# Graph attention on one core: softmax batches of 26 steps, a longer ring of values, and keys and values added in two operations

## The reference, cut to what matters

```python
e = (edge_attr @ We).reshape(-1, H, C)
kj = k[src] + e
vj = v[src] + e
logits = jnp.einsum('ehc,ehc->eh', q[dst], kj) / np.sqrt(C)
m = jax.lax.stop_gradient(jax.ops.segment_max(logits, dst, num_segments=n))
ex = jnp.exp(logits - m[dst])
denom = jax.ops.segment_sum(ex, dst, num_segments=n)
a = ex / (denom[dst] + 1e-16)
agg = jax.ops.segment_sum(vj * a[:, :, None], dst, num_segments=n)
return agg.reshape(n, H * C) + x @ Ws + bs
```

## Time and profile before

| | |
|---|---|
| runs | median 5180.2 us of 3 (5168.29 to 5180.98) |
| the profiled execution's own time | 5169.64 us |
| its span in the profile | 5167.9 us |
| busy share of PE, DVE, ACT, POOL over the span | 85%, 81%, 57%, 60% |
| mean busy share of the DMA engines in e2's steady part | 70% |
| steps of e1 (first to last L1268) | 1365.5 to 3077.4 us |
| steps of e2 (first to last L1268) | 3307.2 to 4972.1 us |

### The profile page before, as it was taken

One profiled execution on the slowest core, in us unless ns is written; L12 is line 12 of the kernel. 1 busy time (PEld: TensorE's weight loads), 2 busy tenths in 40 slices (PEclk: granted clock), 3 DMA queues, 4 the chain that ended last, 5 costly groups with the idle time before them and its releaser, 6 DMA issues. The chain is left out here.

```text
span 5167.9 us, 109620 instructions
## 1 busy us (share of the span) xinstructions
PE 4373.5 (85%) x18094; PEld 3309.7 (64%) x18094; DVE 4191.4 (81%) x21620; ACT 2963.0 (57%) x10810; POOL 3098.8 (60%) x2997
## 2 busy tenths in 40 slices
PE   2666666679899999999999988899999999999978
PEld 1444444445577777777777764577777777777755
DVE  5555555568799999999999986799999999999966
ACT  0000000013188888888888883088888888888881
POOL 5777777710466666666666640476666666666620
PEclk9888787789999999999999997999999999999979
DMA  2444444435677776777776753676677667666734
GB/s 70 120 118 117 118 118 118 118 101 169 191 213 209 206 210 204 211 207 214 208 206 205 206 159 121 198 213 208 206 204 207 204 203 207 205 207 206 207 92 149
DMA packets 573602, 911.16 MB, mean 176 GB/s; under 512 B 93619, under 2 KB 400442, under 8 KB 572935
## 3 DMA queue, kind: packets, MB, share of 16 engines
q0 software_dynamic: 171408, 540.40, 36.2%
q1 hardware_dynamic: 401528, 363.76, 23.2%
HBM read 838.88 MB, written 64.92 MB: 175 GB/s over the span
## 5 line engine op out<-in xcount | busy, mean ns | idle before, releaser
L1162 POOL DMA_INDIRECT e_kv<-kv,src x1664 | 1619.5, 973 | 693.6 <-DVE e_kvj L1268 322.9
L1409 ACT ACTIVATE e_vals<-e_kvj,e_ex 128x65 f32<-128x65 f32 x6656 | 1750.3, 334 | 0.0
L1223 PE MATMUL e_sum<-e_vals,e_mask 128*128 128x260 f32 x3328 | 1077.2, 406 | 217.9 <-ACT e_vals L1409 217.6
L1268 DVE TENSOR_TENSOR e_kvj<-e_kv,e_e 128x512 f32<-128x512 f32 x1664 | 1126.5, 677 | 69.3 <-DMA e_kv<-kv,src 30.3
L1278 DVE CUSTOM_DVE_ANT_0 e_kvj<-e_kvj,e_q 128x64 f32<-128x64 f32 x6656 | 1076.7, 218 | 63.3 <-PE e_q L1184 5.7
L1174 PE MATMUL e_e<-e_we,e_ea 112*128 112x256 f32 x3328 | 1007.9, 384 | 31.4 <-DMA e_ea<-attr_tiles 15.5
L1184 PE MATMUL e_q<-q,e_pick 128*128 x3328 | 999.9, 381 | 26.1 <-POOL e_pick L1152 25.9
L1175 PE MATMUL e_e<-e_we,e_ea 112*128 112x256 f32 x3328 | 990.9, 379 | 0.0
L488 PE MATMUL e_sum<-e_x,e_mask 128*128 x1664 | 583.3, 498 | 403.4 <-DMA e_x<-x_rows,e_src 280.9
L466 POOL DMA_INDIRECT e_x<-x_rows,e_src x783 | 741.5, 947 | 262.4 <-issue 178.8
L1152 POOL TENSOR_SCALAR e_pick<-e_spots,own 128x512 f32<-128x512 bf16 x416 | 657.5, 1581 | 399.1 <-DMA e_spots<-locals 391.2
(11 more groups left out here) (213 smaller groups left out, 3209.4 us busy)
## 6 DMA issues: line engine op xcount, KB each, us to landing
e_ea<-attr_tiles SPq DMA_DIRECT2D x1664, 112.0 KB
e_spots<-locals SPq DMA_DIRECT2D x208, 256.0 KB
e_kv<-kv,src POOLq DMA_INDIRECT x1664
kv<-n_proj_rows SPq DMA_DIRECT2D x98, 256.0 KB
n_x<-x_rows SPq DMA_DIRECT2D x98, 128.0 KB
e_x<-x_rows,e_src POOLq DMA_INDIRECT x783
e_pen<-pens SPq DMA_DIRECT2D x416, 8.1 KB
e_block_cols<-x_cols SPq DMA_DIRECT2D x49, 128.0 KB
```

Of the source, the lines that this page charges most:

```text
L1162: e.indirect_dma_start(out=kv[:, u, :], out_offset=None, **rows_of(kv_rows, k["src"][:, i:i + 1])).then_inc(kv_got[u], 16)
L1223: e.matmul(sums[n % 2][:, 0:VALS], mask[:, n % R, :], vals[:, n % R, :], start=True, stop=True).then_inc(summed, 1)
L1268: e.tensor_tensor(kvj[:, ka:va + 1:va - ka, :, 0:C], kv[:, i % NG, :].rearrange("p (t d) -> p t d", t=2).rearrange(by_head_kv, h=H), pe_e[ ...
L1409: by_weight = e.activation(vals[:, n % R, h * HV:(h + 1) * HV], kvj[:, 2 + n % NV, h, :], ACT.Copy, scale=ex[:, b % 2, h, r:r + 1])
```

## The change

In the attention passes it does the following. A softmax batch has 26 steps instead of 16. LAG follows, from 32 to 42. The ring of values has LAG + 2 buffers instead of LAG + 4, so 44 instead of 36. Keys and values are added by two operations of 256 columns each, with semaphores of their own (`kj_done`, `vj_done`); the dot products wait for the first, the gather and the next product for the second. The destinations are loaded in chunks of 4 steps instead of 8, two chunks ahead. `apart` has one buffer instead of two. Outside the passes, the edge weights (needed in setup and e0 only) lie in the space of the queries.

```diff
-BATCH = 16
+BATCH = 26
...
-    weight = sb("weight", [P, S])
...
-    sb("q", [P, B * D])
+    q = sb("q", [P, B * D])
+    weight = k["weight"] = q[:, 0:S]
...
-    CH, QUAD = 8, 4
+    QUAD = 4
     PACE = 2
     LAG = BATCH + 8 * PACE
-    NV, NG, NE, R = LAG + 4, 6, 6, 4
+    NV, NG, NE, R = LAG + 2, 6, 6, 4
...
-        apart = ph.sb("apart", [P, 2, P])
-        spots = ph.sb("spots", [P, 2, CH * P], BF16)
+        apart = ph.sb("apart", [P, P])
+        spots = ph.sb("spots", [P, 2, QUAD * P], BF16)
...
                 def load_spots(c):
                     if c >= 2:
-                        e.wait_ge(picked, (c - 1) * CH // QUAD)
-                    e.dma_start(spots[:, c % 2, :], locals16[c * CH:(c + 1) * CH, :].rearrange("s c -> (s c)").unsqueeze(0)
-                                .to_broadcast([P, CH * P])).then_inc(spots_got[c % 2], 16)
+                        e.wait_ge(picked, c - 1)
+                    e.dma_start(spots[:, c % 2, :], locals16[c * QUAD:(c + 1) * QUAD, :].rearrange("s c -> (s c)").unsqueeze(0)
+                                .to_broadcast([P, QUAD * P])).then_inc(spots_got[c % 2], 16)
...
-                    if i % CH == 4 and i // CH >= 1 and i // CH + 1 < T // CH:
-                        load_spots(i // CH + 1)
+                    if i % QUAD == 0 and i // QUAD + 2 < T // QUAD:
+                        load_spots(i // QUAD + 2)
...
                     if i >= NG:
-                        e.wait_ge(kvj_done, i - NG + 1)
+                        e.wait_ge(vj_done, i - NG + 1)
...
                     if i >= 2:
-                        e.wait_ge(kvj_done, i - 1)
+                        e.wait_ge(vj_done, i - 1)
...
+                    edge = pe_e[i % 2][:, 0:D].rearrange("p (h c) -> p h c", h=H)
+                    e.tensor_tensor(kvj[:, i % 2, :, 0:C], kv[:, i % NG, 0:D].rearrange("p (h c) -> p h c", h=H), edge,
+                                    ALU.add).then_inc(kj_done, 1)
                     if i >= NV:
                         e.wait_ge(weighed, i - NV + 1)
-                    ka, va = i % 2, 2 + i % NV
-                    by_head_kv = "p t (h c) -> p t h c"
-                    e.tensor_tensor(kvj[:, ka:va + 1:va - ka, :, 0:C],
-                                    kv[:, i % NG, :].rearrange("p (t d) -> p t d", t=2).rearrange(by_head_kv, h=H),
-                                    pe_e[i % 2][:, 0:D].unsqueeze(1).to_broadcast([P, 2, D]).rearrange(by_head_kv, h=H),
-                                    ALU.add).then_inc(kvj_done, 1)
-                    e.wait_ge(kvj_done, i + 1)
+                    e.tensor_tensor(kvj[:, 2 + i % NV, :, 0:C], kv[:, i % NG, D:].rearrange("p (h c) -> p h c", h=H), edge,
+                                    ALU.add).then_inc(vj_done, 1)
+                    e.wait_ge(kj_done, i + 1)
...
-                        if n >= 2:
-                            e.wait_ge(masked, n - 1)
-                        e.activation(apart[:, n % 2, :], k["iota"][:], ACT.Square, bias=k["local"][:, n:n + 1],
+                        if n:
+                            e.wait_ge(masked, n)
+                        e.activation(apart[:], k["iota"][:], ACT.Square, bias=k["local"][:, n:n + 1],
```

More of the change, by code:

```diff
@@ L1066, in edge_pass_attention @@
         w_got, cleared, ones_set = ph.sem("w_got"), ph.sem("cleared"), ph.sem("ones_set")
-        e_done, q_done, kvj_done, dots_done, picked, apart_done = (
-            ph.sem(n) for n in ("e_done", "q_done", "kvj_done", "dots_done", "picked", "apart_done"))
+        e_done, q_done, kj_done, vj_done, dots_done, picked, apart_done = (
+            ph.sem(n) for n in ("e_done", "q_done", "kj_done", "vj_done", "dots_done", "picked", "apart_done"))
         flat_done, lr_done, fw_done, mx_inner = (ph.sem(n) for n in ("flat_done", "lr_done", "fw_done", "mx_inner"))
@@ L1147, in pick_rows @@
                 def pick_rows(c):
-                    e.wait_ge(spots_got[c // 2 % 2], 16 * (c // 4 + 1))
+                    e.wait_ge(spots_got[c % 2], 16 * (c // 2 + 1))
                     if c >= 2:
                         e.wait_ge(q_done, (c - 1) * QUAD)
-                    e.tensor_scalar(pick[:, c % 2, :], spots[:, c // 2 % 2, c % 2 * QUAD * P:(c % 2 + 1) * QUAD * P],
-                                    k["own"][:, 0:1], None, ALU.is_equal).then_inc(picked, 1)
+                    e.tensor_scalar(pick[:, c % 2, :], spots[:, c % 2, :], k["own"][:, 0:1], None, ALU.is_equal).then_inc(picked, 1)
                 e.memset(kvj[:], 1.0).then_inc(ones_set, 1)
@@ L1277, in logits @@
                         hs = slice(h * C, h * C + C)
-                        dot = e.tensor_tensor_reduce(kvj[:, ka, h, 0:C], kvj[:, ka, h, 0:C], pe_q[i % 2][:, hs], 1.0, 0.0,
+                        dot = e.tensor_tensor_reduce(kvj[:, i % 2, h, 0:C], kvj[:, i % 2, h, 0:C], pe_q[i % 2][:, hs], 1.0, 0.0,
                                                      ALU.mult, ALU.add, logit[:, j % 2, h, r:r + 1])
@@ L1404, in _ @@
                             e.wait_ge(summed, n - R + 1)
-                        e.activation(mask[:, n % R, :], apart[:, n % 2, :], ACT.Relu, bias=k["one"][:, 0:1],
+                        e.activation(mask[:, n % R, :], apart[:], ACT.Relu, bias=k["one"][:, 0:1],
                                      scale=-1.0).then_inc(masked, 1)
```

## The result

The changed kernel takes 5004.81 us (median of 4 runs, 4999.59 to 5010.95), the kernel before 5179.05 (4 runs). The ratio is 0.967, with a 95% interval of 0.965 to 0.969. The profiled execution took 5001.25 us, 168.4 less than before. Forecast were 4960, with a range of 4885 to 5060, so the range and the side were right.

What follows compares the result with a forecast made beforehand. PE's 1.74 us plain steps plus 4.38 us once per batch, with DVE's late softmax work behind the large stall, bound the passes; at 1.860 us a step, steady steps plus fill, drain and memset gave -212 us, forecast 4960, range 4885 to 5060.

Steps and rivals of the forecast that it cites:

- Once per batch against plain steps: Attention passes: added steps cost PE's plain 1.74 us, once-per-batch 4.38 us stays, batches fall from 52 to 32 a pass.
- Two adds overlap: DVE's split add: values start 0.34 us after keys, dot products at 0.68, so a step gets 0.04 to 0.05 shorter.
- I take all 1.26: DVE's saving per batch, 0.76 once plus ten times 0.05 us, comes wholly out of PE's waits; bounds 0 and 2.39.
- the rescaling's 0.76: DVE's L1360 moves past the last softmax step, taking 0.76 us off the stretch in which DVE is late.
- PE works about 1.27: PE's once-per-batch work in e2: eight transposes of 0.11 us and 0.38 for the small matmul L1221.
- The smaller stall does not depend on DVE: PE's 0.72 us wait before L1223 after softmax step 7: ACT makes the copy back before it weights.
- the large one: PE's 1.63 us stall before L1223, put down to DVE's late less_max; forecast to shrink to near 1.0.
- the first rival: Stalls stay because the chain is latencies, or the shorter ring offsets the gains: 5033 us, or 5021 for ring; chance 0.25.
- LAG, fill, drain, memset: LAG 42 adds ten fill steps at 1.69 us (1.75 in the first pass), 16.9 us drain per pass, 3.5 us memset altogether.
- Shorter ring at nothing: Values' add waits for ACT's iteration i - 2 instead of i - 4; costs 0 because PE is held too.
- Half chunks at nothing: Destinations issued some 6 steps before their pick instead of 2; ending POOL's 172.8 us wait in e2 is worth 0.
- Signs: Profile after: plain steps 1.74, batch 48.4, e2's steps about 1540 us; wrong if DVE waited for weighed between adds.

Runs made afterwards that it cites:

- e2: Not a run: the second of the kernel's two attention passes; a steady step took 2.014 us in the kernel before, 1.890 in the changed kernel.
- the run with LAG 34: Changed form with batches of 16, LAG 34 and ring of 36 instead of LAG 32: 5344.75 us, ratio 0.982 to the kernel before, against 5317.93 and 0.978.
- the second set: Follow-up runs, among them the unmodified changed kernel, 5223.71 us, ratio 0.961; the kernel before took 5442 us there.

## Why the prediction was right, and where its sum was off

- **Once per batch against plain steps**: right. Plain iterations stayed at 1.74, and what a batch takes beyond 26 of them fell from 4.4 to (1.890 x 26 - 45.24) = 3.9 us, so hardly changed. (The 790 steps hold 30 batches and ten more plain steps, which makes 3.9 a little low; the means by place give 4.5 and 4.1.) Of the sum's -212 us, -136 stood for 20 batches less per pass (with fill, drain and memset) and the rest for DVE's saving. The result of -168 leaves some 32 for the second. No run has the longer batches alone on the first chip; on the later ones they bring 1.8 to 1.9% and the other edits 2.2%, of which half chunks are 1.4%.
- **Two adds overlap**: right, 0.34 and 0.33 from start to start. The page of the Trainium skill that spoke against it (VectorE: DVE Perf Modes, on the errata) asks for 512 elements or more; the durations of 0.41 to 0.42 us fit its formula, but the split gained 0.8% with batches of 26 and cost nothing on the kernel before, so here the measurement decides against the rule. What this case has beside it: the starts of the two adds are 0.34 apart, and the dot products had waited for all of the single add.
- **The term that was mis-sized: "I take all 1.26"**, DVE's saving per batch as it comes out of PE's stalls. By the sum it was to cut 4.38 to 3.12 us; measured were 3.9, so 0.5 in place of 1.26 (0.4 by the means). Two things are in this. Of the 1.26, 0.93 came out of PE's waits in e2. The split's 0.5 is in it: 0.48 in the trace without it, which over 64 batches is 31 of the 41 us. Of the rescaling's 0.76 only a part is, some 0.3 in the run with LAG 34. And moving the rescaling exposed 0.55 us, its small matmul and the wait that it had filled, a term that the sum did not have. "PE works about 1.27" had counted the small matmul as work in its own right, while in the kernel before it stood in a wait.
- **"The smaller stall does not depend on DVE"**: right, 2.46 before and after. But the large one was read one link short. `less_max` does come late, yet ACT's place in line made it PE's stall. With ACT's pieces behind the weighting it goes altogether, with DVE's work unchanged. That bears out half of the first rival, which called this chain one of latencies; its other half, that PE waits whatever DVE saves, does not hold: the split alone took the large stall's iteration from 3.42 to 3.17.
- **LAG, fill, drain, memset**: right, within 2 us each (10.06 us for the memset of 11960 columns against 8.33).
- **Shorter ring at nothing**: right, a buffer more changed nothing beyond noise.
- **Half chunks at nothing**: not borne out where it was tested (1.4%); on the first chip, for which the sum was made, the places of the batch give no sign of it, but it was not run there. On a chip like the later ones this term would have been wrong by 79 us.
- **Rivals**: the result lies between the first (5033) and the forecast (4960), nearer to the first. The range held because the batches' 136 us carry the sum; the part for DVE's saving came out at less than half, for two reasons that the prediction did not have.
- **Signs**: plain steps and the overlap came out as said, POOL's wait went; a batch took 49.1 us instead of 48.4 and e2's steps 1565 instead of 1540. DVE did wait for `weighed` between the adds, which the prediction had called a sign of being wrong, and it cost nothing that shows.

The split alone on the kernel before should have shown some 50 us by the same reasoning and showed none. It ran with chunks of 8, on a chip where these cost time; on top of half chunks, with the shorter ring, it gave 46. That a late chunk took what DVE gained fits this, but how it did is not shown.

## What to carry to other kernels

Split a batch's cost into what comes per step and what comes once per batch before lengthening it, and then ask why the once-per-batch part stalls anybody: here ACT's order in one iteration made it, and moving its three softmax pieces behind the weighting gave 1.9% more on top of the changed kernel, the fastest version of this study (0.942 of the kernel before). When a piece of work moves, look at what it was hiding, not only at what it was delaying. And compare ratios only within a chip: one buffer more looked like 0.5% until the changed kernel ran beside it.

## What the runs showed of the hardware that was not expected

The same changed kernel took 5001 us in the first profile and 5223 in the second set. The record names the chips of the three sets, three different ones with nearly equal times, and not that of the first runs; that the chip makes the difference, and not the hour, is inferred. Most of the difference lies before the attention passes: the first L1264 starts at 1366.3 us on the one and at 1543.3 on the other. The windows of all engines from 50 to 1000 us (PE, PEld, DVE, ACT, POOL busy), of the changed kernel on the first chip and on the other:

```profile
50.00:1000.00 950.00, 574.64 (x1639) 386.42 (x1640) 515.21 (x1534) 0.45 (x2) 701.32 (x739) 0.79 0.40 116
```

```profile
50.00:1000.00 950.00, 504.32 (x1375) 319.80 (x1375) 432.50 (x1290) 0.89 (x4) 593.18 (x625) 0.72 0.34 98
```

PE, DVE and POOL get less done, and the share of the transfers is lower too, 0.34 against 0.40. In the steady part of e2 the changed kernel differs by only 27 us (1519.81 against 1493.13). What holds the first pass back on that chip was not found.
